# An LSTM recurrence behind two attentions on one core: the output gate in a PSUM bank of its own, the low half of h by a scan

## The reference

```
a = xw_t + prev_h @ Wh
i, f, o = sigmoid(a[:, :H]), sigmoid(a[:, H:2H]), sigmoid(a[:, 2H:3H]);  g = tanh(a[:, 3H:])
next_c = f * prev_c + i * g
next_h = o * tanh(next_c)
...
x = x + ffn(hs)
```

## Time and profile before

| | us |
|---|---|
| median of 3 runs | 722.34 |
| lowest, highest | 717.23, 727.45 |
| span of the profiled execution | 717.7 |
| first part and first attention half, to the first gates' tanh | 281.5 |
| recurrence, first ha to last ha | 282.3 to 710.5 |

### The profile page before, as it was taken

One profiled execution on the slowest core, in us unless ns is written; L12 is line 12 of the kernel. 1 busy time (PEld: TensorE's weight loads), 2 busy tenths in 40 slices (PEclk: granted clock), 3 DMA queues, 4 the chain that ended last, 5 costly groups with the idle time before them and its releaser, 6 DMA issues.

```text
span 717.7 us, 13461 instructions
## 1 busy us (share of the span) xinstructions
PE 445.6 (62%) x4970; PEld 316.2 (44%) x4975; DVE 407.0 (57%) x2106; ACT 230.9 (32%) x812; POOL 45.1 (6%) x26
## 2 busy tenths in 40 slices
PE   0113349900655897998889888747467467467436
PEld 0011313400343775666666666536356356356335
DVE  7538303389576684666776776654444444444443
ACT  0014338623333451333343443323222222222222
POOL 9400000343000000000000000000000000000000
PEclk9997569965696996579998999855555555555555
DMA  3488850000000100000000000000000000000000
GB/s 74 16 28 28 101 127 1 2 0 0 0 1 4 27 2 0 2 1 2 1 2 1 3 2 1 3 1 1 5 1 5 6 1 5 5 1 5 5 1 5
DMA packets 10469, 8.56 MB, mean 12 GB/s; under 512 B 1976, under 2 KB 8736, under 8 KB 10404
## 3 DMA queue, kind: packets, MB, share of 16 engines
q1 hardware_dynamic: 9364, 7.19, 10.3%
q10 hardware_dynamic: 1040, 0.52, 0.3%
HBM read 4.03 MB, written 0.52 MB: 6 GB/s over the span
## 4 chain that ended last, share of the span: by engine, by line
PE 42%; DVE 31%; ACT 11%; SPq 10%; issue 5%; DMA 1%; another core or an unknown queue 0%; DVEq 0%
PE bank L1348 14%; ACT th L641 6%; SPq L385 5%; DVE ha L999 4%; DVE pr L992 4%; PE bank L1182 4%; ACT gates L639 4%; DVE gates L996 3%; DVE q_sq L922 3%; DVE mx L915 3%; PE bank L1068 2%; PE bank L1056 2%; PE bank L1309 2%; PE bank L1291 2%; DVE so L994 2%
## 5 line engine op out<-in xcount | busy, mean ns | idle before, releaser
L1348 PE MATMUL bank<-ha,wha 128*128 128x4 f16 x1020 | 67.7, 171 | 123.6 <-DVE ha L999 120.2
L1348 PEld LDWEIGHTS bank<-ha,wha 128*128 128x128 f16 x1020 | 49.3, 105 | 168.5 <-DVE ha L999 165.0
L639 ACT ACTIVATE gates<-bank 128x16 f32<-128x16 f32 x256 | 46.9, 183 | 197.6 <-PE bank L1348 195.1
L992 DVE SCALAR_TENSOR_TENSOR pr<-gates 128x8 f32<-128x8 f32 x256 | 42.9, 167 | 112.2 <-ACT gates L639 112.2
L641 ACT ACTIVATE th<-gates 128x4 f32<-128x4 f32 x256 | 52.6, 205 | 110.1 <-DVE gates L996 110.1
L999 DVE TENSOR_TENSOR ha<-so,th 128x4 f16<-128x4 f32 x256 | 41.4, 162 | 69.6 <-ACT th L641 69.6
L1182 PE MATMUL bank<-kT,qz 128*128 128x128 f32 (+1 forms) x256 | 68.2, 381 | 0.1
L1348 PE MATMUL bank<-hb,wha 128*128 128x4 f16 x1020 | 66.3, 169 | 0.0
L1348 PE MATMUL bank<-ha,whb 128*128 128x4 f16 x1020 | 62.1, 165 | 0.0
L608 ACT ACTIVATE p_mla<-bank,mx 128x128 f32<-128x128 f32 (+1 forms) x128 | 44.5, 414 | 18.1 <-DVE mx L915 18.1
L1003 DVE TENSOR_TENSOR hb<-v_tm,ha 128x4 f16<-128x4 f32 x256 | 41.7, 163 | 8.9
(11 more groups left out here) (218 smaller groups left out, 713.8 us busy)
## 6 DMA issues: line engine op xcount, KB each, us to landing
ada<-ada SPq DMA_DIRECT2D x4, 256.0 KB, 29.9
qz<-qz SPq DMA_DIRECT2D x16, 64.0 KB, 2.0
x_tm<-in_x ACTq DMA_DIRECT2D x1, 512.0 KB, 4.5
ada<-ada SPq DMA_DIRECT2D x4, 128.0 KB, 13.2
wf<-in_L_cond_w_f SPq DMA_DIRECT2D x2, 256.0 KB, 4.6
x_tb<-in_x SPq DMA_DIRECT2D x4, 128.0 KB, 2.7
qz<-qT SPq DMA_DIRECT2D x16, 32.0 KB
out_y<-tb SPq DMA_DIRECT2D x7, 64.0 KB, 1.9
```

What stands on the lines that cost most here:

```text
L639: nc.scalar.activation(gates[:, k, 0:GW], src, ACT.Tanh, scale=1.0 / A_SCALE).then_inc(gates_act, 1)
L992: V.scalar_tensor_tensor(pr[:, k, :], gates[:, k, B:3 * B], 1.0, gates[:, k, 3 * B:5 * B], ALU.add, ALU.mult).then_inc(p_ready, 1)
L1348: ins = T.matmul(acc[:, g * B:(g + 1) * B], w[:, g, :], h, start=False, stop=True, skip_group_check=True)
```

## The change

The output gate moves to a PSUM bank of its own. `inner_bank(c)` holds 12 columns per step (i, f, g) in banks 6 and 7; `out_bank(c)` holds the 4 of gate o for four chunks, in bank 5 for chunks 0 to 3 and bank 4 for chunks 4 to 7. Within a step the high products of the three inner gates go first, then those of gate o, then the low ones of the inner gates (signal `gates_mm`), then the low one of gate o (signal `out_mm`). ScalarE makes two tanh, one over 12 columns and one over 4. The so product follows the new cell state, and waits for the second tanh.

The low half is made by one `tensor_tensor_scan` over slots of three elements per column: the factors are 0, th, so, and the offsets -1, 0, high; the running value becomes 1, then th, then so·th - high, which is the low half. It reads the high half just written and no longer hist, which comes behind it.

Since out_bank(c+1) mostly is the bank that ScalarE reads for gate o, the inputs of the next chunk wait for `out_act` in each of their three steps. The transposes of the second attention half go to columns 128 to 255 of bank 4, and the values there wait for `mo_normed`. Parts 0 to 4 of chunk 0 move behind the first attention half.

```
-                    add(wha, ha[:, k, :])
-                    add(whb, ha[:, k, :])
+                    add(wha, high, inner)
+                    add(whb, high, inner)
+                    add(wha, high, out_gate)
+                    add(whb, high, out_gate)
                     pe.wait_ge(hb_ready, t)
-                    add(wha, hb[:, k, :]).then_inc(gates_mm, 1)
+                    add(wha, low, inner).then_inc(gates_mm, 1)
+                    add(wha, low, out_gate).then_inc(out_mm, 1)
...
-                nc.scalar.activation(gates[:, k, 0:GW], src, ACT.Tanh, scale=1.0 / A_SCALE).then_inc(gates_act, 1)
+                nc.scalar.activation(gates[:, k, B:GW], inner, ACT.Tanh, scale=1.0 / A_SCALE).then_inc(gates_act, 1)
+                act.wait_ge(out_mm, t + 1)
+                nc.scalar.activation(gates[:, k, 0:B], out_bank(t // STEPS)[:, t % STEPS], ACT.Tanh, scale=1.0 / A_SCALE).then_inc(out_act, 1)
...
-                V.tensor_scalar(so[:, k, :], gates[:, k, 0:B], 1.0, 0.5 * H_SCALE, ALU.add, ALU.mult)
                 vec.wait_ge(p_ready, t + 1)
                 V.scalar_tensor_tensor(gates[:, 1 - k, 4 * B:5 * B], pr[:, k, B:2 * B], 0.5, pr[:, k, 0:B], ALU.mult, ALU.add).then_inc(c_new, 1)
+                vec.wait_ge(out_act, t + 1)
+                V.tensor_scalar(h_fac[:, k, :, 2], gates[:, k, 0:B], 1.0, 0.5 * H_SCALE, ALU.add, ALU.mult).then_inc(so_ready, 1)
+                vec.wait_ge(so_ready, t + 1)
                 vec.wait_ge(th_act, t + 1)
-                V.tensor_tensor(ha[:, k, :], so[:, k, :], th[:, k, :], ALU.mult).then_inc(h_ready, 1)
-                hs = hist[:, t, :]
-                V.tensor_tensor(hs, so[:, k, :], th[:, k, :], ALU.mult).then_inc(hist_ready, 1)
-                vec.wait_ge(hist_ready, t + 1)
-                V.tensor_tensor(hb[:, k, :], hs, ha[:, k, :], ALU.subtract).then_inc(hb_ready, 1)
+                V.tensor_tensor(h_off[:, k, :, 2], h_fac[:, k, :, 2], h_fac[:, k, :, 1], ALU.mult).then_inc(h_ready, 1)
+                vec.wait_ge(h_ready, t + 1)
+                V.tensor_tensor_scan(h_low[:, k].rearrange("p b s -> p (b s)"), h_fac[:, k].rearrange("p b s -> p (b s)"),
+                                     h_off[:, k].rearrange("p b s -> p (b s)"), 0.0, ALU.mult, ALU.subtract).then_inc(hb_ready, 1)
+                V.tensor_tensor(hist[:, t, :], h_fac[:, k, :, 2], h_fac[:, k, :, 1], ALU.mult).then_inc(hist_ready, 1)
...
+                    if g > FIRST_UNITS:
+                        pe.wait_ge(mo_normed, g - 1 + (m - FIRST_UNITS) % 2)
...
-            inputs_of(0, range(0, 5))
...
-            inputs_of(0, range(5, 9))
+            inputs_of(0, range(0, 9))
...
                 if t % STEPS in INPUTS_AT and t < S - STEPS:
+                    yield lambda: pe.wait_ge(out_act, t + 1)
                     yield lambda: inputs_of(t // STEPS + 1, range(*INPUTS_AT[t % STEPS]))
```

More of the change, by code:

```diff
@@ L323, in flat, with inner_bank, out_bank, back_bank @@
             return a.rearrange("p t n -> p (t n)")
+        def inner_bank(c):
+            return bank[:, 6 + c % 2, 0:STEPS * 3 * B].rearrange("p (t g b) -> p t g b", g=3, b=B)
+        def out_bank(c):
+            at = (c % 4) * STEPS * B
+            return bank[:, 5 - c // 4, at:at + STEPS * B].rearrange("p (t b) -> p t b", b=B)
+        def back_bank(g):
+            return bank[:, 5, 0:P] if g < FIRST_UNITS else bank[:, 4, P:2 * P]
         UNITS = [(0, g, b, 0) for g in range(NG) for b in range(B)]
@@ L633, in _ @@
                 k = t % 2
-                src = bank[:, 6 + (t // STEPS) % 2, (t % STEPS) * GW:(t % STEPS + 1) * GW]
+                inner = inner_bank(t // STEPS)[:, t % STEPS].rearrange("p g b -> p (g b)")
                 if t == 0:
@@ L957, in _ @@
             m_norm(FIRST_UNITS - 1)
+            go(V.memset(h_fac[:], 0.0))
+            go(V.memset(h_off[:], 0.0))
             step(V.memset(gates[:], 0.0), c_new)
+            done()
+            step(V.memset(h_off[:, :, :, 0], -1.0))
             m_oT(0)
@@ L1232, in inputs_of, with of_gate @@
             def inputs_of(c, parts):
-                acc = bank[:, 6 + c % 2, :]
-                by_gate = acc.rearrange("p (t g b) -> p t g b", g=4, b=B)
+                def of_gate(g):
+                    return out_bank(c) if g == 0 else inner_bank(c)[:, :, g - 1, :]
+                hot = gate_cols[:].rearrange("r (t g b) -> r t g b", g=4, b=B)
                 cols = slice(c * P, (c + 1) * P)
@@ L1237, in inputs_of @@
                     if i == 0:
[L1238 removed]
+                        T.matmul(inner_bank(c), bg_rows[:], hot[:, :, 1:4, :], start=True, stop=True, skip_group_check=True)
+                        T.matmul(out_bank(c), bg_rows[:], hot[:, :, 0, :], start=(c % 4 == 0), stop=True, skip_group_check=True)
                     elif i <= 4:
[L1240 removed]
+                        T.matmul(of_gate(i - 1), wx[:, i - 1, :], xT[:, cols], start=False, stop=True, skip_group_check=True)
                     else:
@@ L1243, in inputs_of @@
                             pe.wait_ge(moT_ready, (1, 2, None, None, 4)[c])
-                        T.matmul(by_gate[:, :, i - 5, :], wox[:, i - 5, :], oT[:, cols], start=False, stop=True, skip_group_check=True)
+                        T.matmul(of_gate(i - 5), wox[:, i - 5, :], oT[:, cols], start=False, stop=True, skip_group_check=True)
             pe.wait_ge(ld_xtb, 64)
@@ L1341, in _, with add @@
                 k = (t + 1) % 2
-                acc = bank[:, 6 + (t // STEPS) % 2, (t % STEPS) * GW:(t % STEPS + 1) * GW]
+                in_acc, out_acc = inner_bank(t // STEPS)[:, t % STEPS], out_bank(t // STEPS)[:, t % STEPS]
                 if t:
                     pe.wait_ge(h_ready, t)
-                def add(w, h):
-                    for g in range(4):
-                        ins = T.matmul(acc[:, g * B:(g + 1) * B], w[:, g, :], h, start=False, stop=True, skip_group_check=True)
+                def add(w, h, gs):
+                    for g in gs:
+                        ins = T.matmul(out_acc if g == 0 else in_acc[:, g - 1], w[:, g, :], h, start=False, stop=True, skip_group_check=True)
                     return ins
+                inner, out_gate = range(1, 4), range(0, 1)
                 if t == 0:
-                    add(wh, h0[:]).then_inc(gates_mm, 1)
-                else:
-                    add(wha, ha[:, k, :])
-                    add(whb, ha[:, k, :])
+                    add(wh, h0[:], inner).then_inc(gates_mm, 1)
+                    add(wh, h0[:], out_gate).then_inc(out_mm, 1)
+                else:
+                    high, low = h_off[:, k, :, 2], h_low[:, k, :, 2]
+                    add(wha, high, inner)
+                    add(whb, high, inner)
+                    add(wha, high, out_gate)
+                    add(whb, high, out_gate)
                     pe.wait_ge(hb_ready, t)
-                    add(wha, hb[:, k, :]).then_inc(gates_mm, 1)
+                    add(wha, low, inner).then_inc(gates_mm, 1)
+                    add(wha, low, out_gate).then_inc(out_mm, 1)
                 for job in pe_jobs(t):
```

16 lines of the change are left out of this document (9 added, 7 removed).

## The result

The changed kernel takes 732.19 us (median of 4 runs, 731.07 to 732.41), beside 722.83 us for the kernel before on the same chip: ratio 1.0142, 95% interval 1.0083 to 1.0202. It is slower, by 1.4%. The forecast was 719 us, so the time is 13 us above it and just outside the range. The profiled span grew from 717.7 to 730.3 us. The first high half of the recurrence starts at 282.26 us (282.32 before), the last at 722.87 (710.54 before): nearly all of the loss, 12.4 us, lies in the 255 periods between them.

What follows compares the result with a forecast made beforehand. The prediction took the 256 recurrence steps to be bound by the latency of a three-engine chain. It summed -10.4 - 0.5 + 6.7 + 0.7 = -3.5 us, forecast 719 us, no change that can be told, range 709 to 731.

Steps and rivals of the forecast that it cites:

- part 1: Recurrence step, a shorter way to the inner gates: first gate matmul to tanh 0.51 against 0.57 us.
- What hides the additions: Second tanh on ScalarE and the moved so product fit in existing waits of the step and cost nothing.
- Gates 0.065 shorter: First gate matmul to inner tanh: 0.065 us gained per clean step, 10.4 us over 160 or so steps.
- The scan 0.18, the low half in time: VectorE's scan takes 0.18 us; up to 0.21 it delays nothing, as TensorE needs the low half at 0.46.
- Rival 2: Slow scan, from high half to low group: over 2% slower from about 0.31 us, 760 us at 0.40; 13%.
- Half of the gain from a low group that starts earlier, 0.03 from one matmul fewer: Gates: low group starts 0.24 instead of 0.27 after the first matmul; tanh waits for one matmul fewer, 0.03.
- Rival 3: TensorE's pace hides the gain: low group not before 0.26, only 0.03 gained per step, 724 to 725 us; 15%.
- VectorE becomes the bound of the steps with a copy or maximum: 64 steps with a 512-element VectorE job: period 1.62 against 1.63 us, 0.5 us gained in all.
- Inputs at the lower clock +5.8: Next chunk's inputs wait for the out gate's tanh: 1.45 us for each of 4 chunks after 460 us.
- Inputs in the attention +0.9: The same wait at full clock, where TensorE has room: 0.3 us for each of 3 chunks.
- rival 1: TensorE's clock falls at the chunk borders amid the attention: 8 to 12 us in all, 727 to 731 us; 25%.
- Junction +0.7: Chunk 0's bias and wx matmuls move behind the first attention half: 1.2 us saved, 1.9 added, net +0.7.

Runs made afterwards that it cites:

- e8: Changed kernel with the two waits ahead of the high half swapped, tanh first and so second: 716.97 us, ratio 0.9935 to the kernel before.
- e1: Changed kernel with the so product back ahead of the cell state, so the high half waits for the tanh alone: 719.09 us, ratio 0.9973.
- e5: Changed kernel with so ahead of the cell state, split inputs, and the low half made as hist less high half, no scan: 720.31 us.
- e6: Kernel before with the scan for the low half and nothing else, one bank and one tanh: 709.74 us, ratio 0.9834.
- e2: Kernel before with an added so signal and a wait for it written ahead of the tanh wait: 745.39 us, ratio 1.0287.
- e10: Kernel before with the added so signal and both waits, the tanh first and so second: 720.73 us, ratio 0.9999.
- e3: Changed kernel with the next chunk's inputs reordered, only matmuls writing the out gate's bank waiting for the second tanh: 724.45 us, ratio 1.0055.
- e4: Changed kernel with both so ahead of the cell state and the input wait only ahead of out-gate matmuls: 707.68 us, ratio 0.9825.

## Why the prediction was wrong

**The step that failed** is in part 1, "What hides the additions": "Both cost nothing. If so were late, ha would slip by as much." so was not late, and the high half slipped by 0.07 all the same. I priced the data's arrival and not the wait that the change adds for it. That wait, written first, moved the late wait for the tanh onto an instruction of its own, 0.07 ahead of the high half; the sum took the last segment of the earlier trace rows, 0.24, over unchanged. 0.07 in each of 255 periods is 17.9 us. It shows fully in the clean steps and hardly where TensorE is the bound (the input periods behind the attention are 32.4 us with it and 32.2 without, in e8); set against the forecast of -3.5 it would give +14.4, where the spans show +12.6. e8, which swaps the two waits and nothing else, gives back 15.2 us; e1, which also moves so, 13.1.

The other steps, in their order:
- *Gates 0.065 shorter.* Right in mechanism, and a little more than said: 0.576 to 0.495 at the lower clock, 0.56 to 0.48 at full clock. Freed from the wait, the 132 late periods gain 9.0 us (e1); 8.3 was forecast.
- *The scan 0.18, the low half in time.* Right: 0.182. Rival 2 is out. The Trainium skill (DVE: opcode table, instruction layouts, handler registers and perf-mode slots; Datapath and trigger behaviour) has it at half throughput. At this size the trace shows no harm from it: 12 elements take some 0.02 us longer than the 4 of the products around it.
- *Half of the gain from a low group that starts earlier, 0.03 from one matmul fewer.* The second is right (0.03, e5 and e6), the first was under-sized: 0.05. Rival 3 is out.
- *VectorE becomes the bound of the steps with a copy or maximum.* Right up to pr (0.37, then no idle time). The period was 1.66 and not 1.62, since it ends in the same slipped segment: 0.70 from pr to the next high half (328.60 to 329.30) instead of 0.64.
- *Inputs at the lower clock +5.8.* Measured +5.2, periods 2.37, 2.25, 2.25. Right.
- *Inputs in the attention +0.9.* Measured +4.0, and the attention's w = 0 and w = 2 lost 4.9 more, of which 0.03 in each of 53 periods, 1.5, is the last segment. The clock fell at all three borders, which the prediction had named as a sign of being wrong. So rival 1 was partly the case: some 6 to 7 us, where I gave it 25% and 8 to 12 us. Its cause, the wait, is not shown alone: the clock also fell at a border in kernels without it.
- *Junction +0.7.* Measured -0.06 at the first high half, but this can't be told from one profile each: with the same code up to there, it starts at 280.31 (e8), 281.24 (e1) and 282.26 us (changed kernel), and at 282.32, 283.47 (e2) and 284.10 (e10) in the old order.
- *Not forecast:* -1.2 us in the first 19 periods, where the clock rose some 6 us earlier than before (308 instead of 314 us).

The range failed for the same reason. It was built from the costs that I had named, and none of the rivals was a cost of the second wait itself, although the change's own lines show it.

Of the experiments' own forecasts the furthest off were e5 (720.3 us, where 711 to 713 were expected) and e6 (709.7, expected 715 to 718). Both had the scan at 0.03 per step, and it is worth 0.05. e6's gain of 13 us on medians is 8.6 from profile to profile (717.7 to 709.1), of which 5.6 lie in the 132 late periods and 3.3 in the first 19, where the clock rose at 302 us instead of 314. The rest is the scatter of the kernel before, 717.23 to 727.45 us, whose profile lies at its low end. Part of that scatter goes with the clock: beside e5 to e8 its fastest run, 716.51 us, had a mean of 0.733 and its slowest, 725.63, one of 0.681. Why e6 (708.67 to 710.95) has little of it was not tested. e1 (2 us above its range), e2 and e3 came out slower than expected too, each with a clock below that of the kernel before in its profile.

## What to carry to other kernels

When a change adds a wait to an instruction on the critical chain, price the wait apart from its data: a semaphore that had come long ago still cost 0.07 us per step here, because the late wait then stood on an instruction of its own, and swapping two lines took it away. Where a VectorE instruction needs two waits, write the one that comes late first, and measure both orders. And put a wait ahead of only those matmuls that need it: whatever stands behind it in TensorE's queue pays (2.25 us against 1.79 in steps 29 and 30 of a chunk at the lower clock, changed kernel and e3). Compare clocks over several executions before you blame a change for a fall.

## What the runs showed of the hardware that was not expected

- The written order of two waits ahead of one VectorE instruction: 0.31 us from the tanh's start to the high half with the late wait second (changed kernel, e2, e3), 0.24 with it first (e8, e10). The wait written second is a sequencer instruction of 21 ns, and the multiply starts 0.07 behind it. The whole time moves by 15.2 us (changed kernel to e8) and 24.7 us (e2 to e10, some 18 of them at like clocks: 738.67 at 0.720 against 719.82 to 721.93 at 0.718 to 0.721).
- At chunk borders in the attention, with TensorE 80 to 90% busy, the clock fell from 1.00 to its lower level in some executions and not in others: at three of three borders in each kernel with the wait ahead of all the inputs, at one or two without it. In the changed kernel it stayed down for seven periods at the first border, and these took 2.8 us more than at full clock in e3.
- A scan over 12 elements per partition costs 0.182 us, as little as a product over 4 with 0.02 on top.
- With the inputs split (e3, e4) the first of a chunk's three periods is still 2.39 us behind the attention, against 1.98 before. It alternates bf16 bias and fp32 products twice, and its wait stands in the middle; whether one of these is the cause was not tested.
